# Gated-delta layer: a chunk's output projection and its addition into x issued one wave later, behind the first squaring

## The reference, cut to what matters

```python
g_cum = jnp.cumsum(gc, axis=-1)
decay = jnp.exp(jnp.tril(g_diff))
L = -jnp.matmul(kbc, jnp.swapaxes(kc, -1, -2), precision=prec) * decay   # strictly lower
attn = solve_triangular(eye - L, jnp.broadcast_to(eye, L.shape), lower=True)
...
v_new = v_i - jnp.matmul(kcd_i, state, precision=prec)
out_i = q_i * exp(g_i) @ state + a_i @ v_new
new_state = state * exp(g_last) + k_i.T @ v_new
...
xf = core * jax.nn.silu(z)
xf = xf * jax.lax.rsqrt(var + EPS) * norm_weight
return xf.astype(hidden_states.dtype).reshape(b, s, VAL_DIM) @ W_out
```

## Time and profile before

| | us |
|---|---|
| median of three executions | 3439.38 |
| profiled execution | 3435.02 |
| its span | 3432.9 |
| TensorE matmul busy | 2990.7 (87%) |
| VectorE busy | 1693.4 (49%) |
| ScalarE busy | 1172.1 (34%) |
| mean granted TensorE clock | 0.884 of full |

### The profile page before, as it was taken

How to read it: one execution, slowest core, us unless ns; L and a number is a source line. 1 busy time by engine, 2 the same in 40 slices (tenths; PEclk the granted TensorE clock), 3 DMA queues, 4 the chain that set the end, 5 groups by cost and what they waited for, 6 DMA issues and landing times. The chain is left out here.

```text
span 3432.9 us, 61371 instructions
## 1 busy us (share of the span) xinstructions
PE 2990.7 (87%) x25380; PEld 1964.0 (57%) x25380; DVE 1693.4 (49%) x3204; ACT 1172.1 (34%) x2299; POOL 225.7 (7%) x219
## 2 busy tenths in 40 slices
PE   6698999699999787848999899899999999999988
PEld 3235444244444334326777777777777777777773
DVE  1633555424443122335556655665566555655651
ACT  2251111133222113123444444444444444444431
POOL 1300111100000100400000000000000000000000
PEclk8898999876555798968999999999999999999998
DMA  1001111000000100000000000000000000000000
GB/s 41 0 0 64 37 37 37 28 0 0 0 0 0 38 5 19 28 25 11 8 11 14 11 8 11 14 11 8 11 14 11 8 14 11 11 14 8 2 5 13
DMA packets 39535, 50.16 MB, mean 15 GB/s; under 512 B 5888, under 2 KB 28672, under 8 KB 39168
## 3 DMA queue, kind: packets, MB, share of 16 engines
q1 hardware_dynamic: 39296, 46.67, 4.2%
HBM read 45.62 MB, written 1.05 MB: 14 GB/s over the span
## 5 line engine op out<-in xcount | busy, mean ns | idle before, releaser
L803 PE MATMUL ps<-all_xn,f_w 128*128 128x512 f32 x640 | 287.9, 595 | 1.9 <-ACT f_share L821 1.9
L1303 PE MATMUL ps<-all_xn,a_w_qkv 128*128 128x512 f32 x512 | 256.1, 625 | 0.0
L1730 DVE SCALAR_TENSOR_TENSOR a_qkv<-a_raw,a_cur_taps,a_qkv 128x1024 f32<-128x1024 f32 x192 | 245.6, 1279 | 1.5
L1397 PE MATMUL ps<-a_inv_half,a_powers 64*64 64x64 f32 x5120 | 219.8, 220 | 0.2 <-DVE a_inv_half L1778 0.2
L1591 ACT ACTIVATE a_powers<-ps 128x512 f32<-128x512 f32 x208 | 124.2, 597 | 260.6 <-PE ps L1389 260.6
L803 PEld LDWEIGHTS ps<-all_xn,f_w 128*128 128x128 f32 x640 | 122.2, 191 | 155.8 <-issue 155.8
L1778 DVE TENSOR_TENSOR a_inv_half<-a_inv_half,ps 128x256 f32<-128x256 f32 x256 | 106.8, 417 | 207.6 <-PE ps L1397 207.6
L1397 PEld LDWEIGHTS ps<-a_inv_half,a_powers 64*64 64x64 f32 x5120 | 186.3, 134 | 11.0 <-issue 10.6
L1711 POOL TENSOR_TENSOR a_rstd<-a_var,a_half 128x4 f32<-128x4 f32 x64 | 64.4, 1007 | 1800.9 <-DVE a_var L1812 1800.9
L826 ACT ACTIVATE f_act_h<-ps 128x512 f32<-128x512 f32 x80 | 47.8, 597 | 375.9 <-PE ps L803 375.9
L569 DVE SCALAR_TENSOR_TENSOR a_score<-a_away,a_slope_cur,ps 128x128 f32<-128x128 f32 (+3 forms) x128 | 69.9, 546 | 214.5 <-PE ps L432 213.9
(11 more groups left out here) (262 smaller groups left out, 5715.8 us busy)
## 6 DMA issues: line engine op xcount, KB each, us to landing
f_w<-in_f_w SPq DMA_DIRECT2D x24, 512.0 KB, 4.6
a_w_qkv<-in_a_w SPq DMA_DIRECT2D x16, 512.0 KB, 3.6
a_w_z<-in_a_w SPq DMA_DIRECT2D x16, 256.0 KB, 2.7
a_w_out<-in_a_wo SPq DMA_DIRECT2D x16, 256.0 KB, 2.7
f_w<-in_f_w SPq DMA_DIRECT2D x24, 128.0 KB, 2.3
f_index_in<-in_f_index SPq DMA_DIRECT2D x1, 2144.0 KB, 12.2
all_x<-in_x_t SPq DMA_DIRECT2D x1, 1024.0 KB, 4.9
a_wq<-in_a_wq SPq DMA_DIRECT2D x2, 512.0 KB, 4.3
```

The source lines that it names most:

```text
L803: mm = pe.matmul(ps[:, bank + n % 2, :], w[:, v, k, f * P:(f + 1) * P], xn[:, k, b * T:(b + 1) * T], start=k == 0, stop=k == KC - 1)
L1303: mm = pe.matmul(ps[:, to, :], w_qkv[:, k, mt * P:(mt + 1) * P], xn[:, k, b * T:(b + 1) * T], start=k == 0, stop=k == KC - 1)
L1397: mm = pe.matmul(halves(BUP)[t, r, :], powers[t, n % 2, u, r, :], inv_half[t, r, :], start=True, stop=True)
L1730: dve.scalar_tensor_tensor(to, rows, tap, to, ALU.mult, ALU.add).then_inc(conv_ready if j == TAPS - 1 else conv_step, 1)
```

## The change

On TensorE `project_out` for chunk w-2 now stands in wave w behind `level(h, w, c, 1)`, ahead of `part`. At the wave's end `join(w)` follows `turn(w + 1)` at once. On VectorE `add_out(w - 2)` stands behind `begin(w)`, and the two convolution taps at the wave's end stand together. The projection of chunk 62, which has no wave 64 to stand in, is issued after the loop; the last chunk's stays where it was. No instruction is added or removed, and no wait.

```diff
@@ TensorE, waves
                         level(h, w, c, 1)
+                        if w >= 2:
+                            project_out((w - 2) // CH, w - 2, (w - 2) % CH)
                         if prepares:
                             part(h, w, c, 0)
...
                         if after:
                             turn(w + 1)
-                        if before:
-                            project_out(bh, w - 1, b)
                         join(w)
@@ TensorE, behind the loop
                 w = CH * KH - 1
+                project_out(KH - 1, w - 1, CH - 2)
                 corner(w, CH - 1)
@@ VectorE, waves
                         begin(w)
+                        if w >= 2:
+                            add_out(w - 2, (w - 2) % CH)
                         if before:
                             make_right(bhp, w - 1, b)
...
-                        taps_of(1)
-                        if before:
-                            add_out(w - 1, b)
-                        taps_of(1)
+                        taps_of(2)
@@ VectorE, behind the loop
                 w = CH * KH - 1
+                add_out(w - 1, CH - 2)
                 make_right(1, w, CH - 1)
```

## The result

The changed kernel takes 3480.31 us in the median of four executions (3470.58 to 3486.59); the kernel before took 3440.28 (3436.06 to 3449.92) beside it. The ratio is 1.011, with a 95% interval of 1.0077 to 1.0143: slower by 1.1%. The forecast was no change (3441, range to 3472). The rival that came closest was "one or more low stretches a head", 3465 with one and 3485 with two.

The account below looks back on a forecast made before the run. TensorE, with two waits a wave for VectorE, was taken to bound the kernel. New waits of 19.2 us, mostly given back at low clock, left +2: 3437 against the profiled 3435.02, 3441 in the median's terms; range 3428 to 3472.

Parts of the forecast that it names:

- one or more low stretches a head: Rival, chance 0.22: new waits bring 1.2 GHz in c = 0 or c = 1; 3465 us, with a second such wave 3485.
- What bounds the kernel: Mid-stage TensorE is busy 456 of 500 us; its losses are waits for `v0` (89.2 us), normed output (58.7), and low clock.
- The new wait: Before the first squaring, TensorE waits for ScalarE's transpose copy: 0.5 us later per border at high clock, 0.25 at low.
- T + 1.39: Forecast squaring start at the high clock, 1.39 us after `turn` starts at a wave border; before the change 2.70 us.
- Edits that cost nothing: Delaying the projection a wave and moving `add_out` (0.69 us) ahead of `make_right` stay hidden, the latter under the `recall` wait.
- What gives it back: Low-clock stretches behind c = 2 and 3 don't move, so lateness halves there; heads stay 112.64 us, +2 instead of 19.2.
- the forecast's equation: Lateness at the `turn` of c = 3, halved by each low stretch: x = ((x + 0.25)/2 + 1.0 + 0.25)/2, giving 0.9 us, not growing.
- The full waits rival: Rival, chance 0.20: low stretches travel with the wave, so every border pays its wait; +19.2 us, 3459.
- The shares of same, slower and faster: Chances of landing inside, above or below the 0.2% band of 3432.5 to 3446.3 us: 0.46, 0.41 and 0.13.
- What would show it: Signs in the later profile: a new `a_vt` wait near 0.5 us before the squaring, old waits unchanged, memset 112.64 us apart.
- the whole working is wrong if the wait is absent: Sign: if the profile has no wait before the first squaring, near 0.5 us at high clock, the whole working fails.
- wrong if the memset's distance moves by more than 1.5 with a lower granted clock: Sign for new low stretches: the once-a-head memset, 112.64 us apart, moves over 1.5 us with granted clock under 0.95.

## Why the prediction was wrong

- **What bounds the kernel**: right. TensorE, two waits for VectorE, the clock as the third loss. That the change leaves the two waits as they were held to 0.1 us, and the kernel that puts the projection under the first shows what that is worth: -9.3 us a head, of which 5.8 are waits (four times 1.44) and the rest clock.
- **The new wait**: right in kind, a little large. The squaring starts at T + 1.31, forecast T + 1.39; with the forecast's own sum that is 1.31 + 1.82 - 2.70 = 0.43 late, forecast 0.51. The term that was too large is the 0.12 from copy to squaring, taken from wave 0. There the squaring stood behind the join: 0.71 from join to squaring is what the join takes at the low clock with the copy long there, as at the end of the wave c = 3 of the earlier trace rows:

```profile
2460.99 0.37 PE L1406 MATMUL ps<-a_inv_half,a_v 64*64 64x64 f32 x1
...
2461.70 0.36 PE L1385 MATMUL ps<-a_v,a_vt 64*64 64x64 f32 x1
```

  Behind the copy itself it is 0.05. A whole wave is only 0.29 longer, since 0.16 comes back at once: the squaring takes 1.08 us and not 1.13 until the next group, and `part`, now behind the projection, 1.81 and not 1.92. At the low clock the squaring starts at T + 1.78, forecast T + 1.84.
- **Edits that cost nothing**: right. VectorE's half and the wave's delay by themselves measure nothing (0.9984 and 0.9991).
- **The step that failed** is "What gives it back": "Then lateness doesn't add up over heads", "a head keeps its length of 112.64 us". It took the low stretches as given in number and length and only asked how much work falls into them. With the new order the head gets 15.36 us of low clock instead of 10.24, longer stretches behind c = 2 and new ones behind c = 0 and 1, and the head goes to 116.05. The sign of the clock's answer was wrong, and it is the larger part, about 2.3 of the 3.4 us. The mechanism itself exists: with 0.45 us less work a head, the head stays at 112.64 with the same 10.24 us of low clock. With the same loss as work elsewhere the head also stays, at 112.65 with 1.14 us more in it, but there because low stretches go (6.8 us), which the forecast's equation doesn't have. With 0.45 us more a head it already fails. I had given more low stretches 0.22 as a rival. The rival's second figure, 3485, was near, in part by luck: it put some 8 us on waits and 36 on two stretches a head, and the stage lost some 18 to lateness and the other 32 to the clock.
- **The full waits rival** (+19) has the right size for the lateness (18) and not for the head.
- **Small sums.** The shares of same, slower and faster add up to 0.47, 0.41 and 0.12 from the parts given, not 0.46, 0.41 and 0.13; a second stretch gives 3483, not 3485. And 0.2% is less than this kernel scatters: its executions beside the runs above lie from 3413.91 to 3451.84 us.
- **The Trainium skill**, "TensorE: Matmul & The Clock Gate", Part 1, holds that the chip judges activity on a beat of its own. Heads that take turns at 115.28 and 116.83 us under a constant program agree. What the forecast drew from it didn't hold. The same page of the Trainium skill, in "Loop structure matters more than you think", speaks against gaps between matmuls, and had the right sign here. The new gaps are 0.20 and about 0.2 us, far shorter than the wait in that section's example, and that they are what brings the low clock isn't shown.
- **What would show it**: no wait for `a_vt` is listed within the waves, since the gap is too short for a row; it shows in the starts. So "the whole working is wrong if the wait is absent" was a sign that couldn't tell: the wait is there and no row has it. The sign "wrong if the memset's distance moves by more than 1.5 with a lower granted clock" is what came.

What stays open: why the new order lengthens the low stretches and not only delays their end. That the amount alone doesn't decide is shown for one amount, by one execution each (the pair with less work; the same loss elsewhere). Since heads answer in steps to small edits, other amounts could come out otherwise, and no run puts the loss as idle time at another place or as dense work right behind the waits in the old order. That the gaps do it, rather than the missing projection between transposes and join, is argued: the join between two halves of the projection has no gap and still 12.3 us of low clock, with a border 0.4 us longer, and with the join first the projection is only 0.8 us later than before, with 13.65; the row of small matmuls rules out only that small matmuls keep the clock low.

## What to carry to other kernels

Before moving work that looks free, ask what it covers where it stands; here 1.8 us of projection hid a copy and a join's input, and the place it went to had nothing to hide. If the program has regular waits just long enough to lower TensorE's clock, a few tenths of a microsecond more next to them can cost several times themselves, and a little less can win nothing (0.45 us a head here, either way): look at the low time per period, not at the waits' sum, and test with a small filler. The work that can be moved belongs under the waits themselves: the same delay by one wave, with the projection put there, was worth 4.1 to 5.1%.

## What the runs showed of the hardware that I had not expected

- A loop's length answered in steps to work put into it: 112.64, 112.64, 114.34 us a head for -0.45, 0 and +0.45 us. Over all kernels with the two waits uncovered the mean heads are 109.59, 112.6, 114.34, 115.35, 116.05, and 119.5 to 119.7.
- From a group of 64x64 matmuls that run in pairs to one with 128x128 weights takes 0.2 us more than to another group of 64x64 (0.61 and 0.41 us from the join's first start to the next group's). Behind the squaring it is 0.1 more: 0.57 to the projection (2272.20 to 2272.77 in the changed kernel) and 0.46 to the next 64x64 group (2278.59 to 2279.05).
- A stretch of low clock followed one in which TensorE had been busy throughout (1950.7 to 1954.1 of the changed kernel, 3.40 of 3.40 us). The stretches of the changed kernel's heads are 3.4 or 6.8 us long; with the join between two halves of the projection some behind c = 3 are 10.2.
- The low clock can vanish: 10.24 us a head before, 1.0 with the projection under the first wait, though the second wait is still there (57.7 us in 62 times between 1600 and 3250).
